# Splitting two long transfers, moving zeros and half of a placing, and leaving the block out of a table-lookup kernel

## The reference, cut to what matters

```python
# x: (64, 64, 512) float32   conditions: (64,) int32 in 1..198   weights: (200, 64, 64) float32
w = weights[conditions]                         # one 64x64 matrix for each of the 64 batches
return x + jnp.einsum('bct,bcd->bdt', x, w)     # b: batch, c: channel, t: 512 columns
```

## Time and profile before

| what | value |
|---|---|
| median of three runs | 48.3 us (47.49, 48.3, 48.56) |
| the profiled execution's own time | 47.52 us |
| its span, first to last instruction | 45.6 us |
| busy: TensorE / VectorE / ScalarE / GpSimd | 23.4 / 14.9 / 14.6 / 2.6 us |
| bytes moved by DMA | 17.83 MB, mean 391 GB/s over the span |
| granted TensorE clock, mean | 0.981 |

### The profile page before, as it was taken

The page is one execution under the profiler, slowest core; times in us unless marked ns, Lnnn a source line. Parts: engine busy times, 40 slices in busy tenths (PEclk is TensorE's granted clock), DMA queues, the critical chain, the costliest instruction groups (busy, mean ns, idle before and its releaser), DMA issues.

```text
span 45.6 us, 301 instructions
## 1 busy us (share of the span) xinstructions
PE 23.4 (51%) x98; PEld 10.0 (22%) x98; DVE 14.9 (33%) x20; ACT 14.6 (32%) x18; POOL 2.6 (6%) x10
## 2 busy tenths in 40 slices
PE   0004000000000009999999789999999999930000
PEld 0004000000000004243527054534534434300000
DVE  0891000000003980009559290064064065550000
ACT  0820000000000009009999999062062063450000
POOL 4080900000000000000000000000000000000000
PEclk9999999999999999999999999999999999999975
DMA  0689999999999999999997999999998999999991
GB/s 0 108 338 431 424 417 431 417 439 424 431 431 511 431 403 417 388 460 460 460 331 280 403 424 453 381 489 446 460 417 338 431 446 403 424 439 388 417 406 47
DMA packets 2162, 17.83 MB, mean 391 GB/s; under 512 B 242, under 2 KB 242, under 8 KB 498
## 3 DMA queue, kind: packets, MB, share of 16 engines
q1 hardware_dynamic: 2016, 16.78, 89.1%
q0 software_dynamic: 144, 1.05, 5.4%
q10 hardware_dynamic: 2, 0.00, 0.0%
HBM read 9.44 MB, written 8.39 MB: 391 GB/s over the span
## 4 chain that ended last, share of the span: by engine, by line
PE 43%; DMA 21%; DVE 10%; ACT 7%; issue 5%; POOL 2%; POOLq 1%
PE product L156 31%; DMA gathered<-weights,table_row 21%; PE product L160 12%; DVE w_all L186 5%; ACT y_sb L116 4%; ACT w_diag L111 3%; POOL w_diag L128 2%; DVE w_diag L168 2%; DVE y_sb L195 2%; DVE gathered L183 1%; POOLq L36 1%; DVE piece L171 0%; DVE one L169 0%
## 5 line engine op out<-in xcount | busy, mean ns | idle before, releaser
L160 PE MATMUL product<-x_sb,w_all 64*64 64x512 f32 x64 | 8.9, 698 | 13.0 <-DVE w_all L186 12.9
L156 PE MATMUL product<-x_sb,w_diag 128*128 128x512 f32 x32 | 14.0, 594 | 0.3 <-issue 0.3
L191 DVE COPY y_sb<-product 128x1024 f32<-128x1024 f32 x7 | 8.6, 1225 | 12.6 <-PE product L156 7.2
L116 ACT COPY y_sb<-product 128x1024 f32<-128x1024 f32 x7 | 7.1, 1012 | 8.5 <-PE product L156 6.3
L111 ACT COPY w_diag<-w_all 64x256 f32<-64x256 f32 x8 | 5.1, 637 | 14.6 <-DVE w_all L186 14.4
L156 PEld LDWEIGHTS product<-x_sb,w_diag 128*128 128x128 f32 x32 | 6.0, 190 | 8.3 <-issue 8.3
L160 PEld LDWEIGHTS product<-x_sb,w_all 64*64 64x64 f32 x64 | 3.5, 207 | 17.6 <-DVE w_all L186 13.0
L183 DVE TENSOR_TENSOR gathered<-gathered,piece 128x64 f32<-128x64 f32 x1 | 0.3, 270 | 10.0 <-DMA gathered<-weights,table_row 10.0
L139 PE MATMUL product<-one,row_along 1*128 1x1 f32 x2 | 0.6, 344 | 3.6 <-DVE row_along L175 3.6
L186 DVE STREAM_TRANSPOSE w_all<-gathered 128x2048 f32<-128x2048 f32 x1 | 2.3, 2311 | 0.0
L195 DVE COPY y_sb<-product 128x512 f32<-128x512 f32 x2 | 1.4, 692 | 1.5 <-PE product L156 1.5
(11 more groups left out here) (4 smaller groups left out, 0.4 us busy)
## 6 DMA issues: line engine op xcount, KB each, us to landing
out<-y_sb SPq DMA_DIRECT2D x5, 1024.0 KB, 6.2
x_sb<-x SPq DMA_DIRECT2D x4, 1024.0 KB, 8.3
x_sb<-x SPq DMA_DIRECT2D x2, 2048.0 KB, 19.9
out<-y_sb SPq DMA_DIRECT2D x1, 2048.0 KB, 6.7
out<-y_sb SPq DMA_DIRECT2D x2, 512.0 KB, 4.3
condition<-conditions ACTq DMA_DIRECT2D x1, 0.2 KB
gathered<-weights,table_row POOLq DMA_INDIRECT x1, 9.7
```

The lines of the kernel that those rows point to most:

```text
L116: nc.scalar.copy(y_sb[:, 4 * turn:4 * turn + 2, :], product[turn % SETS][0][:, :, :]).then_inc(moved_by_act, 1)
L156: product_of = nc.tensor.matmul(product[turn % SETS][j][:, g, :], w_diag[:, n - 4 * TILED, :], x_sb[:, n, :], start=True, stop=True)
L160: product_of = nc.tensor.matmul(product[turn % SETS][h][halves(g), j, :], w_all[halves(h), :, n], x_sb[halves(h), n, :], start=True, stop= ...
L191: nc.vector.tensor_copy(y_sb[:, 4 * turn + 2:4 * turn + 4, :], product[turn % SETS][1][:, :, :]).then_inc(moved_by_dve, 1)
```

## The change

The loads of x become eight transfers of one turn each, and the store of turns (2, 3) becomes two. Zeros of `w_diag` are written by ScalarE, with two copies from a broadcast zero; VectorE sets that zero, and its 64x1024 memset and that of GpSimd go, together with GpSimd's wait for `pieces_set`, which VectorE does later. The placing copies are shared: ScalarE places partitions 0 to 63 and VectorE partitions 64 to 127. The engines' programs stand in the main program, without a block. Cut to its core:

```diff
-    LOADS = [(0, 0), (1, 1), (2, 2), (3, 3), (4, 5), (6, 7)]
-    STORES = [(0, 0), (1, 1), (2, 3), (4, 4), (5, 5), (6, 6)]
+        zero = sbuf("zero", [P, 1], fp32)
-        block = ctx.enter_context(nc.Block())
...
+        def on_sync(sp):
+            for turn in range(TURNS):
+                sp.dma_start(x_sb[:, pairs_of(turn), :], x[:, pairs_of(turn), :]).then_inc(x_loaded[turn], 16)
+            for turn in range(LAST):
+                sp.wait_ge(moved_by_act, turn + 1)
+                sp.wait_ge(moved_by_dve, turn + 1)
+                sp.dma_start(out[:, pairs_of(turn), :], y_sb[:, pairs_of(turn), :]).then_inc(stored, 16)
...
+        def on_scalar(act):
             act.dma_start(condition[:, :, :], conditions).then_inc(condition_loaded, 16)
+            act.wait_ge(zero_set, 1)
+            for h in range(PAIR):
+                nc.scalar.copy(w_diag[halves(h), :, (1 - h) * D:(2 - h) * D],
+                               zero[halves(h), :].unsqueeze(2).to_broadcast([C, PAIRS - 4 * TILED, D])
+                               ).then_inc(w_zeroed, 1)
+            act.wait_ge(w_ready, 1)
             for turn in range(TURNS):
                 if turn < TILED:
-                    later = slice(4 * turn, 4 * turn + 4)
-                    act.wait_ge(w_ready, 1)
-                    for h in range(PAIR):
-                        nc.scalar.copy(w_diag[halves(h), later, h * D:(h + 1) * D],
-                                       w_all[halves(h), :, pairs_of(TILED + turn, TILED + turn)].rearrange("p d n -> p n d")
-                                       ).then_inc(w_placed, 1)
+                    nc.scalar.copy(w_diag[halves(0), pairs_of(turn), 0:D],
+                                   w_all[halves(0), :, pairs_of(TILED + turn)].rearrange("p d n -> p n d")
+                                   ).then_inc(w_placed_by_act, 1)
...
-            pool.wait_ge(pieces_set, 2 * (P // Q))
-            nc.gpsimd.memset(w_diag[halves(1), :, 0:D], 0.0).then_inc(w_zeroed, 1)
...
                 if turn >= TILED:
-                    pe.wait_ge(w_placed, PAIR * (turn - TILED + 1))
+                    pe.wait_ge(w_placed_by_act, turn - TILED + 1)
+                    pe.wait_ge(w_placed_by_dve, turn - TILED + 1)
...
-            nc.vector.memset(w_diag[halves(0), :, D:PAIR * D], 0.0).then_inc(w_zeroed, 1)
+            nc.vector.memset(zero[:, :], 0.0).then_inc(zero_set, 1)
...
+            dve.wait_ge(pieces_set, 2 * (P // Q))
             dve.wait_ge(w_gathered, 16)
...
+            dve.wait_ge(w_ready, 1)
             for turn in range(LAST):
+                if turn < TILED:
+                    nc.vector.tensor_copy(w_diag[halves(1), pairs_of(turn), D:PAIR * D],
+                                          w_all[halves(1), :, pairs_of(TILED + turn)].rearrange("p d n -> p n d")
+                                          ).then_inc(w_placed_by_dve, 1)
...
+        on_sync(nc.sync)
+        on_scalar(nc.scalar)
+        on_gpsimd(nc.gpsimd)
+        on_tensor(nc.tensor)
+        on_vector(nc.vector)
```

More of the change, by code:

```diff
@@ L58, in conditioned_residual_kernel @@
                    for s in range(SETS)]
-        x_loaded = {first: semaphore(f"x_loaded{first}") for first, _ in LOADS}
+        x_loaded = [semaphore(f"x_loaded{turn}") for turn in range(TURNS)]
         condition_loaded = semaphore("condition_loaded")
         one_set = semaphore("one_set")
+        zero_set = semaphore("zero_set")
         rows_along = semaphore("rows_along")
@@ L70, in conditioned_residual_kernel @@
         w_zeroed = semaphore("w_zeroed")
-        w_placed = semaphore("w_placed")
+        w_placed_by_act = semaphore("w_placed_by_act")
+        w_placed_by_dve = semaphore("w_placed_by_dve")
         multiplied = semaphore("multiplied")
@@ L75, in conditioned_residual_kernel, with pairs_of @@
         stored = semaphore("stored")
-        block = ctx.enter_context(nc.Block())
         def halves(h):
             return slice(h * C, (h + 1) * C)
-        def pairs_of(first, last):
-            return slice(4 * first, 4 * last + 4)
+        def pairs_of(turn):
+            return slice(4 * turn, 4 * turn + 4)
         def round_of(turn, j):
             return slice(4 * turn + 2 * j, 4 * turn + 2 * j + 2)
[L87 to L96, removed]
+        def on_sync(sp):
[5 more added lines that the diff above has]
+                sp.dma_start(out[:, pairs_of(turn), :], y_sb[:, pairs_of(turn), :]).then_inc(stored, 16)
             for j in range(2):
@@ L100, in _ @@
                 sp.dma_start(out[:, round_of(LAST, j), :], y_sb[:, round_of(LAST, j), :]).then_inc(stored, 16)
-            sp.wait_ge(stored, 16 * (len(STORES) + 2))
-        @block.scalar
-        def _(act):
+            sp.wait_ge(stored, 16 * (TURNS + 1))
+        def on_scalar(act):
             act.dma_start(condition[:, :, :], conditions).then_inc(condition_loaded, 16)
+            act.wait_ge(zero_set, 1)
[4 more added lines that the diff above has]
+            act.wait_ge(w_ready, 1)
             for turn in range(TURNS):
                 if turn < TILED:
-                    later = slice(4 * turn, 4 * turn + 4)
-                    act.wait_ge(w_ready, 1)
-                    for h in range(PAIR):
-                        nc.scalar.copy(w_diag[halves(h), later, h * D:(h + 1) * D],
-                                       w_all[halves(h), :, pairs_of(TILED + turn, TILED + turn)].rearrange("p d n -> p n d")
-                                       ).then_inc(w_placed, 1)
+                    nc.scalar.copy(w_diag[halves(0), pairs_of(turn), 0:D],
+                                   w_all[halves(0), :, pairs_of(TILED + turn)].rearrange("p d n -> p n d")
+                                   ).then_inc(w_placed_by_act, 1)
                 if turn < LAST:
@@ L121, in _, with on_gpsimd @@
                 nc.scalar.copy(y_sb[:, 4 * LAST + 2 * j, :], product[LAST % SETS][j][:, 0, :]).then_inc(moved_by_act, 1)
-        @block.gpsimd
-        def _(pool):
+        def on_gpsimd(pool):
             for q in range(P // Q):
                 nc.gpsimd.memset(piece[q * Q:(q + 1) * Q, 0:1], float(1 - q % K)).then_inc(pieces_set, 1)
-            pool.wait_ge(pieces_set, 2 * (P // Q))
-            nc.gpsimd.memset(w_diag[halves(1), :, 0:D], 0.0).then_inc(w_zeroed, 1)
             pool.wait_ge(rows_known, 1)
@@ L132, in _, with on_tensor @@
                                          ).then_inc(w_gathered, 16)
-        @block.tensor
-        def _(pe):
+        def on_tensor(pe):
             pe.wait_ge(one_set, 1)
@@ L142, in _ @@
             for turn in range(TURNS):
-                if turn in x_loaded:
-                    pe.wait_ge(x_loaded[turn], 16)
+                pe.wait_ge(x_loaded[turn], 16)
                 if turn >= SETS:
@@ L164, in _, with on_vector @@
                         product_of.then_inc(multiplied, 1)
-        @block.vector
-        def _(dve):
-            nc.vector.memset(w_diag[halves(0), :, D:PAIR * D], 0.0).then_inc(w_zeroed, 1)
+        def on_vector(dve):
+            nc.vector.memset(zero[:, :], 0.0).then_inc(zero_set, 1)
             nc.vector.memset(one[:, :], 1.0).then_inc(one_set, 1)
```

## The result

The change did not make the kernel faster. It took 48.22 us (48.13 to 48.41, six executions) against 47.88 (47.49 to 48.56, six) of the kernel before: 1% slower, ratio 1.010, interval 1.005 to 1.015. The forecast was 47.6. Ratios here leave out executions over 1.5% above the fastest of their kernel, on both sides; where an event splits the executions of a kernel, its count is given too. In a second measurement, on another chip, the changed kernel was at 47.92 us, ratio 1.002 (0.999 to 1.005). So the 1% did not come back there; what both measurements show is that the forecast gain is missing.

A forecast was written before the change was run, and what follows sets the result against it. The DMA queue, full at 428 GB/s, was taken as the bound: 47.52 - 0.4 (block's end) + 0.1 (8 KB runs) = 47.2 us; the median gave 48.0, the middle 47.6, range 46.9 to 48.4.

The forecast's parts named there:

- the prediction's own signs of being wrong: Last landing moved over 0.5 us, a store landing 1.8 us plus its bytes after issue, or time outside the span changed.
- The bound: Whole kernel: the DMA queue decides, full at 428 GB/s; compute matters only where a store comes too late.
- The sum 47.2: Whole kernel: profiled 47.52 us, less 0.4 for the block's end, plus 0.1 for shorter runs.
- later weights: Possible reason for longer runs, through the store (2, 3) without slack; the change would remove it; left undecided.
- None of it shortens the time: the queue is full, the bytes are the same. It turns into slack: Earlier compute, TensorE's turn 4 starting 1.2 us earlier, gives no time, only 1.5 us of slack at store 6.
- the passage: From last load to first store, 23 to 25 us: 0.50 us lost at 320 GB/s; shorter packets gain 0 to 0.5, taken 0.
- The 1.92 us outside the span I leave as they are: After the span: time unchanged; removing the block's end saves 0 to 0.4 us inside the span, taken 0.4.
- 8 KB runs: Loads and stores of one turn: a loss of 0 to 0.15 us on 6.3 MB, taken as 0.1.
- Store of turn 2 alone: Issued at some 25.2 us, not 28.62; gives the queue some 3 us, under 0.1 us back in this execution.
- The start: VectorE's 0.91 us memset goes, so line 175, gather and turn 0 come 0 to 0.9 us earlier, taken 0.4.
- The placing: One placing to VectorE at 0.5 us; turns 0 to 3 take 8.5 us in place of 9.3.
- Rivals D and E: D: slow VectorE placing, late from 1.3 us, 49.3 us, 3%. E: transfers not overlapping at seams, 52.6 us, 2%.

The follow-up runs named there:

- zeros alone: The kernel before with only the zeros of `w_diag` written by ScalarE, the memsets of lines 128 and 168 out: 48.02 us, 1.003.
- block restored: The changed kernel with the engines' five functions put back in a block, nothing else: 48.34 us, 1.0135 to the kernel before.
- changed, six waits fewer: The changed kernel with all placings waited for once ahead of turn 4, six waits fewer on TensorE: 47.35 us, 0.988 to the kernel before.
- placing alone: The kernel before with only the placing shared between ScalarE and VectorE: 0.996 from the six faster of twelve executions, median of all 47.96 us.
- 8 KB runs alone: The kernel before with loads and stores of one turn each, nothing else: 47.71 us, 1.001.
- block out: The kernel before without its block, nothing else: 47.35 us, 0.988.
- block out, 8 KB runs: The kernel before without its block and with loads and stores of one turn each, zeros and placing as before: 46.69 us, 0.977; again 46.96 us, 0.979.
- held by a load: The changed kernel with SP waiting for the load of turn 6 before the first store: 0.974 from four of twelve executions, median of all 47.42 us.
- held by turn 1: The changed kernel with the first store also waiting for the moves of turn 1: median of all eight 46.78 us, 0.974 to the kernel before.
- held by turn 1, six waits fewer: The changed kernel with the first store held until turn 1 is moved and six waits fewer on TensorE: 46.59 us, 0.970 to the kernel before.
- eight waits on TensorE: The kernel before without block and with one-turn loads and stores, plus eight waits more on TensorE's queue: 49.05 us, 1.027.

## Why the prediction was wrong

The profiled executions differ by 0.7 us (47.52 to 48.20). Some 0.5 us of it lies ahead of the last landing, and 0.2 behind it. The 0.2 is worked out from two terms: leaving the block out gave 1.0 us, judged by the kernel without block and without fetch, which ends 1.3 us after its last landing; and some 1.2 us came back with the late fetch. Of the prediction's own signs of being wrong one came, the time outside the span went from 1.9 to 2.4 us, and another, a last landing moved by over 0.5 us, stood at its edge.

**The bound was right.** The DMA queue decides: the last move ended 1.0 us earlier and the time didn't follow.

**The start of the forecast.** The sum 47.2 was moved up to 47.6 because of a median of 48.3, from three executions. Six gave 47.88. The spread that the prediction put down to later weights, with doubt, looks like the late fetch's: the longer executions of the kernel before have its two signs.

**The step that failed** is "None of it shortens the time: the queue is full, the bytes are the same. It turns into slack", together with taking 0 for the passage, "between 0 and a gain of 0.5". A loss was excluded without a reason. It measured 0.63 us, and 0.5 at the last landing. The earlier compute put the first store into the queue earlier, while loads were running, and the last loads slowed down. The profiled executions, by issue of the first store, with GB/s from 22 to 25 us (the six not listed have a first store from 22.48 to 22.96 and 415 to 426):

| kernel | first store at | GB/s |
|---|---|---|
| zeros alone | 20.88 | 317 |
| block restored | 21.08 | 325 |
| changed, second time | 21.12 | 322 |
| changed, six waits fewer | 21.18 | 336 |
| changed | 21.24 | 336 |
| before | 21.79 | 344 |
| placing alone | 22.18 | 410 |
| 8 KB runs alone | 22.23 | 418 |
| block out | 22.32 | 407 |
| block out, 8 KB runs | 22.33 | 421 |
| held by a load | 22.88 | 426 |
| held by turn 1 | 23.24 | 418 |
| held by turn 1, six waits fewer | 23.95 | 396 (queue empty for a moment) |

The kernel before stood on this slope itself (the rate of its window is also moved by how its 16 KB packets are counted); the dip that I read in the earlier trace rows and set aside as "the last load passes to the first store" was the sign of it. Its chance of 0 to 0.5 us of gain was real, and needed a later store, not shorter runs. My use of "store 0 was waiting then, so it isn't starvation" was right and stopped one question short: waiting was the harm.

**"The 1.92 us outside the span I leave as they are"** failed twice. Leaving the block out gives up to 1.0 us, not 0.4: beside the 0.4 us of the span, the time outside falls from between 1.8 and 2.1 to between 1.3 and 1.5. I argued that the runtime's own barrier of the Trainium skill (Runtime: NRT & Kernel Launch, "The ~15µs preamble/postamble breakdown") comes in addition; that agrees with the sign, though no run shows that barrier by itself, and the size was read from the span alone. And with more waits on TensorE comes the late fetch of instructions: 0.5 us and more outside the span, or 1.6 us and more in it. The same page of the Trainium skill ("Instruction fetch mechanics") says that engines stream instructions in blocks of 16 KB and that crossing a boundary is mostly hidden. The packet here has that size; that it is hidden doesn't hold when it comes among the last stores, and seems not to hold after them.

**8 KB runs**: taken at 0.1 us, measured 1.001 alone. **Store of turn 2 alone**: store (2, 3) was rightly seen as the place without slack; in the kernel without block its pause was 0.43 us and went with the 8 KB runs, when the ratio went from 0.988 to 0.977. **The start**: I took 0.4 us, the bounds 0 to 0.9; the gather came 1.2 us earlier, since line 175 began 0.4 us earlier and its two instructions also fell from 1.06 to 0.28 us together. The prediction wrote that GpSimd's memset "saves nothing", but before it ran beside line 175, from 2.39 to 3.35 us; where it is gone, line 175 is short. As VectorE's own memset went with it each time, the cause isn't shown. **The placing**: 0.40 us for the 0.5 taken. It gave 0.7 us in turns 2 and 3, and TensorE's slow pace in turns 0 and 1 took as much back: 9.25 us and not 8.5, so turn 4 came 0.9 us earlier and not 1.2. **Rivals D and E** didn't occur: a placing took 0.40 us and not 1.3, and three more transfers cost nothing that 1.001 shows. (The 2.0 us cited from the Trainium skill, DMA: Bandwidth & Descriptors, "Anatomy of one DMA — SWDGE (gpsimd) path", are for transfers that GpSimd issues; those in question are issued by SP.) The slow side that did occur was none of mine.

**Open:** why a waiting store slows the loads ahead of it; whether the fetch comes by the length of TensorE's program or by when its instructions run (a held store changed its frequency too, without a change to TensorE); what it costs after the span, apart from the other differences; and whether the longer executions of the kernel before have it, as their signs say, since the packet was seen with the block in two other kernels only.

## What to carry to other kernels

When one DMA queue is full, ask of every step that comes earlier what it puts into the queue ahead of time: loads and stores in one queue can cost more together than one after the other, and a store may have to be held until the loads are nearly through. Compare the execution's own time with the last landing, not the spans alone. After an edit that adds instructions, even waits that are long fulfilled, look first at what they take on their own engine, then past the end of the span for packets of instructions, and count the executions that show them.

## What the hardware did unexpectedly

- A store that joined the queue at 20.9 us, some 3 us before the loads could be done, went with 317 GB/s from 22 to 25 us, against 426 with the store at 22.9, and with the engines counted as busy in both; from 22.2 us on there was next to no loss.
- One 16 KB packet of instructions of 0.93 us on one DMA engine made that engine finish its last stores 1.6 us (held store) and 1.8 us (eight waits on TensorE) after the others.
- Eight fulfilled waits on TensorE took 0.6 us ahead of turn 0, and cost 2.4 us of the time in one kernel and 0.8 in another, by where the late fetch fell. The same eight in idle time of VectorE cost nothing.
